# Block update in groups of ten, and last visits interleaved with the second projection, in a two-layer graph network

## The reference, cut to what matters

```
y  = silu(concat(h, agg) @ uW1 + ub1) @ uW2 + ub2
x1 = layernorm(x + (h + y))            # h is x: row = 2 x + y
m  = segment_sum(x1[src], dst) / max(count, 1)
out = layernorm(x1 + relu(m @ W.T + b))
layernorm(v) = (v - mean) / sqrt(var + 1e-5)
```

## Time and profile before

| | |
|---|---|
| median of three runs | 4301.83 us (4300.47 to 4306.43) |
| the profiled execution | 4298.34 us, span 4296.2 us |
| busy share of the span | TensorE 75%, its weight loads 55%, VectorE 62%, ScalarE 35%, GpSimd 70% |
| granted TensorE clock, mean of the span | 0.889 of full speed |
| chain that ended last | GpSimd 35%, TensorE 21%, issue 20%, DMA 15%, VectorE 5% |

### The profile page before, as it was taken

The page is one execution under the profiler, slowest core; times in us unless marked ns, Lnnn a source line. Parts: engine busy times, 40 slices in busy tenths (PEclk is TensorE's granted clock), DMA queues, the critical chain, the costliest instruction groups (busy, mean ns, idle before and its releaser), DMA issues.

```text
span 4296.2 us, 78474 instructions
## 1 busy us (share of the span) xinstructions
PE 3223.5 (75%) x16047; PEld 2355.4 (55%) x16048; DVE 2682.6 (62%) x11914; ACT 1494.8 (35%) x2712; POOL 3005.4 (70%) x2631
## 2 busy tenths in 40 slices
PE   7657777777777777777777777879577777777775
PEld 3246666566656665666665666658444444444444
DVE  6356666666666666666666666858754555554555
ACT  2225545555545555554555555643100000000004
POOL 0258888888888888888888888751277777777734
PEclk9879989999999999998989899999788888888898
DMA  4665555555555555555555555585433333333324
GB/s 147 193 194 93 95 93 94 94 94 94 93 95 92 95 93 95 92 95 93 94 93 95 94 93 94 77 159 157 132 105 104 104 104 104 105 104 104 105 58 119
DMA packets 336078, 455.16 MB, mean 106 GB/s; under 512 B 53568, under 2 KB 282524, under 8 KB 335772
## 3 DMA queue, kind: packets, MB, share of 16 engines
q0 software_dynamic: 199680, 327.32, 41.6%
q1 hardware_dynamic: 116844, 105.48, 8.6%
q10 hardware_dynamic: 19248, 19.66, 1.3%
HBM read 296.41 MB, written 155.62 MB: 105 GB/s over the span
## 4 chain that ended last, share of the span: by engine, by line
POOL 35%; PE 21%; issue 20%; DMA 15%; DVE 5%; SPq 1%; ACT 1%; DVEq 1%; ACTq 0%; POOLq 0%
POOL sum L560 19%; POOL arena L549 14%; PE ps L846 9%; DMA arena<-x_tab,esrc 9%; DMA sum<-arena,sidx 3%; PE ps L849 3%; PE ps L800 2%; POOL arena L590 2%; PE ps L749 2%; DMA arena<-x_tab 1%; PE ps L712 1%; DMA arena<-loc_tab 1%; PE ps L818 1%; PE ps L736 1%; DVE arena L1526 1%
## 5 line engine op out<-in xcount | busy, mean ns | idle before, releaser
L560 POOL DMA_INDIRECT sum<-arena,sidx x832 | 1317.5, 1584 | 293.5 <-issue 248.7
L549 POOL DMA_INDIRECT arena<-p_tab,esrc x832 | 811.6, 975 | 448.4 <-issue 420.7
L590 POOL DMA_INDIRECT arena<-x_tab,esrc x832 | 794.4, 955 | 304.4 <-issue 146.0
L846 PE MATMUL ps<-arena 128*125 x1760 | 664.4, 465 | 340.2 <-DMA arena<-x_tab,esrc 298.3
L749 PE MATMUL ps<-w,arena 128*128 128x256 f32 x3328 | 838.5, 385 | 3.9 <-ACT arena L967 3.9
L846 PEld LDWEIGHTS ps<-arena 128*125 128x125 f32 x1760 | 380.1, 226 | 607.1 <-issue 521.0
L1325 DVE TENSOR_TENSOR arena<-ps,arena 128x256 f32 x880 | 373.5, 424 | 538.5 <-DMA arena<-p_tab,esrc 308.0
L1526 DVE TENSOR_TENSOR arena<-ps,arena 125x257 f32 x880 | 374.6, 426 | 507.0 <-PE ps L846 473.8
L749 PEld LDWEIGHTS ps<-w,arena 128*128 128x128 f32 x3328 | 571.8, 192 | 122.0 <-issue 5.2
L722 PE MATMUL ps<-ident,arena 128*128 128x128 f32 x1664 | 276.5, 320 | 461.1 <-DVE arena L1357 461.0
L712 PE MATMUL ps<-arena 128*128 128x256 f32 x1664 | 519.9, 469 | 2.7 <-ACT arena L957 2.5
(11 more groups left out here) (186 smaller groups left out, 3977.5 us busy)
## 6 DMA issues: line engine op xcount, KB each, us to landing
arena<-loc_tab SPq DMA_DIRECT2D x220, 125.0 KB
arena<-sum SPq DMA_DIRECT2D x200, 128.0 KB, 2.1
sum<-scr ACTq DMA_DIRECT2D x3, 6400.0 KB, 57.7
arena<-p_tab,esrc POOLq DMA_INDIRECT x832, 3.0
sum<-arena,sidx POOLq DMA_INDIRECT x832
arena<-x_tab,esrc POOLq DMA_INDIRECT x832, 2.8
sum<-scr SPq DMA_DIRECT2D x1, 6400.0 KB, 23.5
arena<-x_tab SPq DMA_DIRECT2D x50, 128.0 KB, 2.0
```

The source lines that it names most:

```text
L549: pool.indirect_dma_start(out=ring0[:, tile % RING, :], out_offset=None, in_=p_tab[:, :], in_offset=bass.IndirectOffsetOnAxis(ap=esrc[:, t ...
L560: pool.indirect_dma_start(out=sums[u][:, :], in_=tot[:, par, u, :], in_offset=None, out_offset=bass.IndirectOffsetOnAxis(ap=sidx[:, par, u ...
L590: pool.indirect_dma_start(out=ring[:, tile % LATER_RING, 0:D], out_offset=None, in_=x1_tab[:, :], in_offset=bass.IndirectOffsetOnAxis(ap=e ...
L846: nc.tensor.matmul(ps[0:NB, u, 0:CW], same1[:, par, u, :], ring[:, bass.ds(at[u], 1), :].rearrange("p a c -> p (a c)"), start=True, stop=T ...
```

## The change

It has two halves.

In the block update the loops of VectorE, ScalarE and SyncE go by ten blocks (`group_loop`). VectorE has `group_scales`, the chain of `block_scales` over the ten blocks of one group plus one operation that makes the shift (`shiftb`), in the fifth step of the next ten. ScalarE normalises two blocks of the group in each of the steps six to ten (40 blocks of groups 0 to 3, and five of group 4); VectorE normalises the last five after the loop. SyncE stores group g-2 in the sixth load step of group g (GROUP_STORE_AT is 5); the last two groups are stored behind the loop. TensorE's and GpSimd's code of this stage stays as it was.

In layer 1 the 12 last quads leave the visit loops. TensorE does each of them visit by visit with up to four blocks' columns and projection between them, without the product L849; the blocks are those that are complete by then (`whole_blocks`), 13 steps. VectorE does the reciprocals by the step (4 blocks), the next one-hots, and after each accumulation the result and statistics of one block of the step before; after each tenth block it runs `group_scales`. ScalarE normalises blocks 0 to 44, 18 blocks behind its column move, VectorE the last five; GpSimd normalises none. SyncE stores groups 0, 1 and 2 behind its loads of blocks 29, 39 and 49, and groups 3 and 4 at the end.

```diff
+        GROUPS = BLOCKS // GROUP
...
+        def group_loop(eng, lag, step):
+
+            for j in range(GROUP):
+                step(j, j, 0)
+            with eng.Fori(1, GROUPS) as g:
+                for j in range(GROUP):
+                    step(g * GROUP + j, j, g)
+            for j in range(lag):
+                step(BLOCKS + j, j, GROUPS)
...
+        TAIL_QUADS = QUADS - TILE_QUADS
+        TAIL = TAIL_QUADS + 1
+        SHARE = BLOCKS - GROUP // 2
+
+        def whole_blocks(j):
+
+            return range(max(0, QT * j - 2), min(BLOCKS, QT * j + 2))
...
-            steps(sp, BLOCKS, 0, load_0)
...
-            for g in range(BLOCKS // GROUP):
-                sp.wait_ge(k[0]["norm"], GROUP * (g + 1))
-                store(g, x1_tab[0:N, :], s_x1st)
...
+            def load_and_store(q, j, g):
+                load_0(q, j % 2)
+                if j == GROUP_STORE_AT and not (isinstance(g, int) and g < 2):
+                    sp.wait_ge(k[0]["norm"], (g - 1) * GROUP)
+                    store_x1(g - 2)
+            for g in range(2):
+                for j in range(GROUP):
+                    load_and_store(g * GROUP + j, j, g)
+            with sp.Fori(2, GROUPS) as g:
+                for j in range(GROUP):
+                    load_and_store(g * GROUP + j, j, g)
+            sp.wait_ge(k[0]["norm"], (GROUPS - 1) * GROUP)
+            store_x1(GROUPS - 2)
+            sp.wait_ge(k[0]["norm"], (GROUPS - 1) * GROUP + LAST_ACT)
+            sp.wait_ge(s_lastnorm, GROUP - LAST_ACT)
+            store_x1(GROUPS - 1)
...
-            sp.wait_ge(e[1]["acc"], QUADS * QT)
-            steps(sp, BLOCKS, 0, load_1)
-            for done, count, g in NORM_ORDER:
-                sp.wait_ge(s_norm1[done], count)
-                store(g, out, s_out)
+            for q in range(BLOCKS):
+                load_1(q, q % 2)
+                if q % GROUP == GROUP - 1 and q >= 3 * GROUP - 1:
+                    g = q // GROUP - 2
+                    sp.wait_ge(s_norm1["act"], GROUP * (g + 1))
+                    store(g, out, s_out)
+            sp.wait_ge(s_norm1["act"], BLOCKS - GROUP)
+            store(BLOCKS // GROUP - 2, out, s_out)
+            sp.wait_ge(s_norm1["act"], SHARE)
+            sp.wait_ge(s_norm1["dve"], BLOCKS - SHARE)
+            store(BLOCKS // GROUP - 1, out, s_out)
...
-            pool.wait_ge(s_shift, 1)
-            for q in range(4 * GROUP, 5 * GROUP):
-                nc.gpsimd.tensor_scalar(rows[0:NB, q, 0:D], rows[0:NB, q, 0:D], momb[:, 1, q:q + 1],
-                                        nwb[:, 3, q:q + 1], ALU.subtract, ALU.mult).then_inc(s_norm1["pool"], 1)
...
+                    if not isinstance(q, int) or q < TILE_QUADS:
+                        nc.tensor.matmul(ps[:, PK, :], identh[:, :],
+                                         identh[:, :].unsqueeze(1).to_broadcast([P, QT, P]), start=True, stop=True)
+                    beside(u)
...
-            for q in range(TILE_QUADS, QUADS):
-                aggregate(q, q % WIDE)
...
-            pe.wait_ge(e[1]["acc"], QUADS * QT)
-            for q in range(BLOCKS + 1):
-                block_1(q, q % 2)
+            for j in range(TAIL):
+                pe.wait_ge(e[1]["acc"], QT * (TILE_QUADS + j))
+                own = list(whole_blocks(j))
+
+                def beside(u):
+                    if u < len(own):
+                        block_1(own[u], own[u] % 2)
+                if j < TAIL_QUADS:
+                    aggregate(TILE_QUADS + j, (TILE_QUADS + j) % WIDE, beside)
+                else:
+                    for u in range(QT):
+                        beside(u)
+            block_1(BLOCKS, BLOCKS % 2)
...
+            def normalise_rows(q):
+                row = rows[0:NB, bass.ds(q, 1), 0:D].rearrange("p a d -> p (a d)")
+                nc.scalar.activation(row, row, ACT.Identity, bias=shiftb[:, bass.ds(q, 1)],
+                                     scale=nwb[:, 3, bass.ds(q, 1)]).then_inc(t["norm"], 1)
+
+            def block_and_rows(q, j, g):
+                block_0(q, j % 2)
+                first = isinstance(g, int) and g < 1
+                if j >= GROUP // 2 and not first:
+                    if j == GROUP // 2:
+                        ac.wait_ge(s_scaled, g)
+                        ac.sem_inc(s_turn_act, 1)
+                    done = g * GROUP - GROUP + 2 * (j - GROUP // 2)
+                    for i in range(2):
+                        if not (isinstance(g, int) and done + i >= BLOCKS - GROUP + LAST_ACT):
+                            normalise_rows(done + i)
+            group_loop(ac, GROUP, block_and_rows)
...
-            steps(ac, BLOCKS, 1, block_1, by=4)
...
-            ac.wait_ge(s_shift, 2)
-            for g in (2, 3):
-                for q in range(g * GROUP, (g + 1) * GROUP):
...
+            BEHIND_ROWS = GROUP + 8
+            for q in range(BLOCKS + BEHIND_ROWS):
...
+                    columns_1(q, q % 2)
                 if live(q - 1, BLOCKS):
...
+                    mean(q - 1, (q - 1) % 2)
+                if live(q - BEHIND_ROWS, SHARE):
+                    normalise_rows(q - BEHIND_ROWS)
...
+            def group_scales(g):
+                own = bass.ds(g * GROUP, GROUP)
+                m, n = 7 * g, g * NEWTON_OPS
+                dve.wait_ge(t["stat"], (g + 1) * GROUP)
+                dve.sem_inc(s_turn_dve, 1)
+                nc.vector.tensor_tensor(momb[:, 0, own], bstb[:, own, 1], bstb[:, own, 4], ALU.subtract)\
+                    .then_inc(t["mom"], 1)
+                nc.vector.tensor_tensor(momb[:, 1, own], bstb[:, own, 1], bstb[:, own, 4], ALU.add)\
+                    .then_inc(t["mom"], 1)
+                nc.vector.tensor_tensor(momb[:, 2, own], bstb[:, own, 2], bstb[:, own, 5], ALU.add)\
...
+                    .then_inc(t["mom"], 1)
+                dve.wait_ge(t["mom"], m + 7)
+                inverse_root(dve, momb[:, 2, own], [nwb[:, i, own] for i in range(4)], t["newt"], n)
+                dve.wait_ge(t["newt"], n + NEWTON_OPS)
+                nc.vector.scalar_tensor_tensor(out=shiftb[:, own], in0=momb[:, 1, own], scalar=-1.0, in1=nwb[:, 3, own],
+                                               op0=ALU.mult, op1=ALU.mult).then_inc(s_scaled, 1)
...
-            steps(dve, BLOCKS, 5, block_0, by=4)
-            block_scales()
-            with dve.Fori(0, BLOCKS // GROUP) as g:
-                for j in range(GROUP):
-                    normalise(g * GROUP + j, t["norm"])
+
+            def block_and_scales(q, j, g):
+                block_0(q, j % 2)
+                if j == 4 and not (isinstance(g, int) and g < 1):
+                    group_scales(g - 1)
+            group_loop(dve, 5, block_and_scales)
+            for q in range(BLOCKS - GROUP + LAST_ACT, BLOCKS):
+                normalise(q, s_lastnorm)
...
-            steps(dve, QUADS, 0, step_1, ahead=1, by=4)
+            steps(dve, TILE_QUADS, 0, step_1, ahead=1, by=4)
...
-            dve.wait_ge(s["acc"], QUADS * QT)
-            nc.vector.tensor_scalar(cnt[:, 0, :], rows[0:NB, :, D], 1.0, None, ALU.max).then_inc(t["cnt"], 1)
-            dve.wait_ge(t["cnt"], 1)
-            nc.vector.reciprocal(cnt[:, 1, :], cnt[:, 0, :]).then_inc(t["cnt"], 1)
...
-            steps(dve, BLOCKS, 0, block_1, by=4)
-            block_scales()
...
-            for q in range(2 * GROUP):
+            def counts(j):
+                own = whole_blocks(j)
+                a, z = own[0], own[-1] + 1
+                dve.wait_ge(s["acc"], QT * (TILE_QUADS + j))
+                nc.vector.tensor_scalar(cnt[:, 0, a:z], rows[0:NB, a:z, D], 1.0, None, ALU.max).then_inc(t["cnt"], 1)
+                dve.wait_ge(t["cnt"], 2 * j + 1)
+                nc.vector.reciprocal(cnt[:, 1, a:z], cnt[:, 0, a:z]).then_inc(t["cnt"], 1)
...
+            def whole_row(q):
+                result(q, q % 2, 1)
+                if q % GROUP == GROUP - 1:
+                    group_scales(q // GROUP)
+            for j in range(TAIL + 1):
+                if j < TAIL:
+                    counts(j)
+                before = list(whole_blocks(j - 1)) if j > 0 else []
+                if j < TAIL_QUADS:
+                    if j + 1 < TAIL_QUADS:
+                        one_hot_1(TILE_QUADS + j + 1, (j + 1) % 2)
+                    accumulate(TILE_QUADS + j, j % 2, lambda u: whole_row(before[u]) if u < len(before) else None)
+                else:
+                    for q in before:
+                        whole_row(q)
+            for q in range(SHARE, BLOCKS):
                 normalise(q, s_norm1["dve"])
```

101 lines of the change are left out of this document (68 added, 33 removed).

## The result

| | before | after |
|---|---|---|
| median | 4301.2 us (4300.47 to 4306.43, 4 runs) | 4276.63 us (4274.15 to 4279.53, 4 runs) |
| profiled execution | 4298.34 us, span 4296.2 us | 4274.15 us, span 4272.4 us |
| granted TensorE clock, mean | 0.889 | 0.888 |

The account below looks back on a forecast made before the run. TensorE was taken to bound the block update, then an exposed border, GpSimd's gathers and an exposed end. 4298.3 + 8.5 - 4 - 18.8 = 4284.0 profiled, 4287.5 as median, rounded 4288 us; range 4265 to 4312.

Parts of the forecast that it names:

- Part A, added: Block update: four group_scales delay TensorE's tables 5.0 us each, less 0.3 slack, plus 1.8 for clock: 26 us added.
- first rival: Block update: scales in the loop cost only 3.0 each, clock stays, 12 us in place of 26: 4274; chance 0.20.
- the second (39 us): Block update: scales or held-back loads at their worst, 9.8 us a group, +39 in place of 26: 4301; chance 0.13.
- Part A, removed: Last statistics to first gather: only group 4's scales, rows and store stay, 15.5 to 15.8 against 33.3: 17.5 us saved.
- part C: The end, from row 49's start: only groups 3 and 4 left to store, 17.6 against 36.4: 18.8 us saved.
- One store is 20.34 / 5 = 4.1 of issue: Border before the gathers: one group's store takes 4.1 us of issue, then landing takes 5.3.
- The stores in SyncE's loop at no cost: Block update: a store delays the next load by 2.6 us, just the slack, and the scales delay its user too: nothing.
- Part B: Last visits beside the projection: 112 us against 115.9, 4 us saved, bounds 18 saved and 10 lost.
- VectorE is just the slower one: Last visits: VectorE needs 6.85 us a step, TensorE 6.6.
- 14 us for coupling: Last visits: load waits 0.5 in ten steps, slow clock 1.2 four times, last eight rows at 1.4 for 0.92.
- The fourth rival: Last visits: engines' steps chained end to end, no overlap, 10 us lost in place of 4 won: 4301; chance 0.07.
- The third rival: Last visits: without the L849 products TensorE keeps losing its clock, 5.8 us more a step, six steps: 4322; chance 0.10.

Follow-up runs that it names:

- the kernel with filler: The changed kernel with 18 identity products on TensorE ahead of the block whose tables come late, into a bank nobody reads: 4270.15 us, ratio 0.9919.
- the one-hots' 4.4 us: Kernel with block update scales spread and stores in pairs, its last visits' one-hots moved from ahead of the first accumulation to behind the second: 4265.17 us, 0.9900.

## Why the prediction was right, and where not

The direction, and which part gains and which loses, came out as forecast; 4276.63 us lies 11 us below the number, about half of that from one term. Of the four signs that the forecast named, two came (the stands with a low clock behind them, and row 49 at 108.7 us for "some 110"); the other two, about 16 us at the border and 17 to 18 at the end, were 13.1 and (from the start of row 49) 15.4, both for the most part by that term.

**Part A, added: 24.5 us for the forecast 26.** The mechanism is as forecast; that the number fits so well is in part luck. The scales hold the tables back 4.5 us, for 5.0: the register work adds 0.64 us to the chain (4.00 us in the loop, 3.36 behind it), not 1.7, so that most of it hides; 0.27 more come from the first operation starting 0.42 behind the statistics and not 0.15. The clock costs 1.7 in two groups and 3.0 in the others, 2.3 in the mean, for 1.8 that were taken from the restart in the earlier trace rows; the kernel with filler shows it as a cause. The two errors cancel, 26.5 us in four groups for 26, and the 2 us that the bare loop was quicker are in no term. The first rival (cheap scales, 12 us, clock unharmed) and the second (39 us) are both excluded by the stage. That the lump as such is the price was argued from VectorE's slack of 0.3 us and is shown by spreading it: without the lump 17.4 us go.

**Part A, removed: 20.6 for 17.5, and part C: 21.0 for 18.8. Here a step failed:** "One store is 20.34 / 5 = 4.1 of issue". The row of 20.34 us for ten issues is not the cost of issuing. The trace of before shows it already where the merged row is taken apart (shortest, median and longest of the ten issues in ns):

```profile
L463 SPq DMA_DIRECT2D x_tab<-arena x10: 317/1820/3027, 3063.5 to 3080.9; - x10
```

The first group's two issues took 0.35 and 0.56 us, the last group's 1.61 and 3.03. The burst is 17.2 us of issuing, most of it with data of earlier stores still on their way, and 3.1 between issues, most of that waiting for rows. One group's store by itself takes 0.93 to 1.1 us. At the 252 to 301 GB/s that were moved from 3064 to 3084, 1.25 MB (10 x 125 x 256 x 4 bytes) take 4.3 to 5.1 us (an estimate); they belong to the transfer, where the forecast had 4.1 on top of a landing of 5.3: measured 6.5 for both, not 9.4. In part C 2.3 for 4.2, for the same reason; there group 3's store, begun 5.5 us earlier, lies close ahead. These are 3.1 of the 9.5 us between -14.3 and -23.8 at the border, and 2.2 at the end.

**The stores in SyncE's loop at no cost:** right for this kernel, and for the reason named (the kernel with stores behind its loop: 196.8 against 197.0). But the slack alone, of 2.6 us, did not suffice, as the forecast had it "just": it reckoned with an issue of 4.1 us ahead of the loads, but the issue took 1.04, and what the loads waited for were the store's data. The uncovered price is 5.8 us in three groups, 1.7 to 2.0 each as waits. The forecast's question, what it costs if the cover is gone, was answered there with up to 4.1 a group.

**Part B, -7.2 for -4,** well inside the bounds of 18 saved and 10 lost. "VectorE is just the slower one" holds in five of the eleven steps: 6.5 us bare for 6.85, without a wait for TensorE. The four lumps at 3.3 measured 3.4, and a slow clock after them was there (0.66 from 4200 to 4210). But the 14 us for coupling were not made up as forecast. VectorE's waits for loads in the eleven steps come to one of 0.2 us, for the 0.5 in each of ten steps; the slow clock cost more than 1.2 a time, 1.8, 3.1 and 1.6 us over a bare step. The reading of the one-hots as plain work for VectorE left out that they cover TensorE's first visit. What the last eight rows gave was not taken apart, so how far the closeness is luck stays open. The fourth rival fell with the stretch's 108.7.

**The third rival,** the clock lost for good without the L849 product, fell: the mean over the last visits was 0.92, and putting the product back changed the ratio by nothing.

**Two differences belong to no term:** the 1.7 us between the last gather and the last gathered visit, which no experiment explains (in the fourteen profiles that stretch takes 7.2 to 9.9 us, whatever was changed, so it may be chance), and the 2.5 us of an earlier start in the profile of before.

**A version that beats both kernels** is the changed one with spread scales in the block update and x1 stored by pairs of blocks: 4248.29 us beside 4300.75, 0.9874 (0.9857 to 0.9890), 1.3% faster than before where the change alone brought 0.6%. Stores behind the loop (0.9881) are as good.

## What to carry to other kernels

Moving work out of an exposed border into a loop pays only if the loop's full engine does not see it. A serial chain of tiny operations is best spread one by one behind the large operations of the engine that carries it: by the length of the stage the 20 operations cost 6.1 us a group as a lump, and with the stores out of the way 0.3 spread. Read the issue time of several large DMAs behind each other one by one: in a burst it holds the time of the data before, and is no price per issue. Work at a step's start can be worth its place, if it covers another engine's first result. And an edit that costs nothing under a stall should be priced again when the stall is removed.

## What the runs showed that I had not expected

- A store of 1.25 MB in two DMAs issues in 0.93 to 1.1 us alone, and in 20.34 us for five in one burst, of which the first takes 0.9 and the last 4.7.
- Five such stores, the first of them begun 17 us ahead of the last statistics, delayed the first gather by nothing: border 13.1 us with one store or with five behind the loads.
- A chain of dependent operations on 10 columns takes 4.00 us with addresses from a register and 3.36 with fixed ones, though each register instruction by itself is 57 to 88 ns.
- Behind four stands of the same length (4.14 to 4.18 us) the clock stayed low for different times: they cost 3.0, 1.7, 3.0 and 1.7 us of TensorE's work.
- Forty-eight more full-width products in the last visits left the time as it was; the granted clock rose from 0.92 to 0.98, and the two cancelled.
- The start of the block update, behind unchanged code, varies by 10 us from profile to profile (2881.1 to 2891.2), a good part of the differences that these edits make. Without stretches cut at events the one-hots' 4.4 us would have looked like 11.
